# Two edits in a two-layer transformer kernel: the table of expert slots made on PE with gathered rows, and two gate groups of the LSTM's second block made at its entry

## The reference, cut to what matters

```python
gates = softmax(tokens @ wg)                        # 2048 x 8
expert_idx = argmax(gates)                          # one expert per token
pos = cumulative count of the token in its expert - 1
keep = pos < capacity                               # capacity 320 = 1.25 * 2048 / 8
y = gate * (relu(x @ w1[e] + b1[e]) @ w2[e] + b2[e])   # 0 for tokens that are not kept
out = residual + y
```

## Time and profile before

| | us |
|---|---|
| median of 3 runs (737.61 to 740.12) | 737.67 |
| profiled execution | 740.06 |
| its span, first to last instruction | 738.0 |
| PE busy | 683.7 (93%) |
| DVE busy | 437.1 (59%) |
| ACT busy | 343.8 (47%) |
| POOL busy | 132.9 (18%) |

### The profile page before, as it was taken

One profiled execution on the slowest core, in us unless ns is written; L12 is line 12 of the kernel. 1 busy time (PEld: TensorE's weight loads), 2 busy tenths in 40 slices (PEclk: granted clock), 3 DMA queues, 4 the chain that ended last, 5 costly groups with the idle time before them and its releaser, 6 DMA issues.

```text
span 738.0 us, 16775 instructions
## 1 busy us (share of the span) xinstructions
PE 683.7 (93%) x6616; PEld 573.8 (78%) x6625; DVE 437.1 (59%) x1152; ACT 343.8 (47%) x938; POOL 132.9 (18%) x220
## 2 busy tenths in 40 slices
PE   6699999999999999979999998999999999798992
PEld 2487778888889988867776776899999999434772
DVE  5499857748756657699999996333343444400321
ACT  1589852333222222378888885355554544101331
POOL 3225730140000000043000010000000000061576
PEclk8899999999999999999999998999999999789997
DMA  7600300000000000124222000000000000213222
GB/s 245 187 20 17 133 2 1 1 1 1 1 1 1 1 1 1 47 67 94 67 70 77 25 4 2 2 1 1 1 3 1 1 2 1 57 40 91 18 20 20
DMA packets 30007, 24.46 MB, mean 33 GB/s; under 512 B 3826, under 2 KB 27123, under 8 KB 29555
## 3 DMA queue, kind: packets, MB, share of 16 engines
q1 hardware_dynamic: 26482, 21.40, 10.2%
q0 software_dynamic: 3456, 2.12, 2.1%
HBM read 17.96 MB, written 5.80 MB: 32 GB/s over the span
## 4 chain that ended last, share of the span: by engine, by line
PE 81%; DVE 9%; issue 4%; SPq 3%; ACT 2%; DMA 1%; POOL 0%; POOLq 0%; DVEq 0%; ACTq 0%
PE SC L670 15%; PE PT L680 12%; PE MI L597 5%; PE SC L854 5%; PE PT L587 5%; PE SC L524 4%; PE SC L578 3%; PE SC L775 3%; PE SC L946 2%; PE SC L814 2%; PE SC L778 2%; PE SC L819 2%; PE PJ L560 2%; PE SC L781 2%; PE PT L825 2%
## 5 line engine op out<-in xcount | busy, mean ns | idle before, releaser
L1066 ACT ACTIVATE big<-SC 128x512 f32<-128x512 f32 x88 | 52.5, 598 | 144.3 <-PE SC L670 144.3
L680 PEld LDWEIGHTS PT<-wd,big 128*128 128x128 f32 (+1 forms) x768 | 90.2, 191 | 2.5 <-issue 0.4
L680 PE MATMUL PT<-wd,big 128*128 128x128 f32 (+1 forms) x768 | 90.6, 274 | 0.0
L1401 DVE TENSOR_TENSOR big<-SC,big 128x512 f32<-128x512 f32 (+1 forms) x88 | 60.5, 689 | 41.6 <-PE SC L670 32.3
L670 PE MATMUL SC<-xP,wgP 128*128 128x512 f32 x264 | 78.8, 406 | 0.7 <-DVE big L1401 0.3
L670 PE MATMUL SC<-xP,wuP 128*128 128x512 f32 x264 | 74.4, 390 | 0.0
L597 PEld LDWEIGHTS MI<-vblk,PTs 128*64 128x64 f32 x1536 | 49.8, 139 | 11.1 <-ACT oT L1013 2.8
L670 PEld LDWEIGHTS SC<-xP,wuP 128*128 128x128 f32 x264 | 49.5, 188 | 10.8
L597 PE MATMUL MI<-vblk,PTs 128*64 128x18 f32 x1536 | 54.2, 213 | 3.9 <-ACT big L1018 1.7
L524 PE MATMUL SC<-warm 128*128 128x512 bf16 x169 | 46.9, 432 | 9.5 <-DVE guess L1204 4.7
L1008 ACT ACTIVATE PTs<-PT 128x512 f32<-128x512 f32 x96 | 52.2, 595 | 7.6 <-PE PT L587 6.5
(11 more groups left out here) (227 smaller groups left out, 1323.1 us busy)
## 6 DMA issues: line engine op xcount, KB each, us to landing
kvs<-in_ctxT SPq DMA_DIRECT2D x32, 64.0 KB, 2.0
w1s<-in_e1w SPq DMA_DIRECT2D x8, 256.0 KB, 2.8
w2s<-in_e1w SPq DMA_DIRECT2D x8, 256.0 KB, 3.1
wg<-in_wg SPq DMA_DIRECT2D x1, 1408.0 KB, 9.2
wu<-in_wu SPq DMA_DIRECT2D x1, 1408.0 KB, 12.1
slots_in<-big SPq DMA_DIRECT2D x1, 1300.0 KB, 5.3
big<-slots_in SPq DMA_DIRECT2D x8, 130.0 KB, 2.4
wd<-in_wd SPq DMA_DIRECT2D x2, 512.0 KB, 14.2
```

The source lines that it names most:

```text
L680: last = pe.matmul(PT[:, e % 2, t * P:t * P + P], h[0:w, t * P:t * P + P], wd[0:w, e, c, :], start=(c == 0), stop=(c == 2))
L1066: act.activation(sg[a % 2], SC[:, a % 2, :], ACT.Silu).then_inc(s["silu_done"], 1)
L1401: last = dve.tensor_tensor(hT[e % 2][0:w, c, :], SC[0:w, 2 + a % 2, :], sg[a % 2][0:w, :], ALU.mult)
```

## The change: what it does

**Second block's gates.** At the entry PE also makes groups 0 and 1 of block 1, in the banks `PT[:, 0]` and `PT[:, 1]`, where six warming matmuls stood. ACT copies them in step 0. Step 1 makes group 2 and step 2 group 3, like all other blocks. In step 0 two warming matmuls go.

**Table of slots.** The slot number minus an offset is split in two: its block of 128 (`in_block`, a one-hot over `NQ` = 20 blocks) and its lane in the block (`at_lane`, a one-hot over 128 lanes, 16 tiles in four pieces of four). POOL multiplies `in_block` by the token's number (minus 4096) and by its gate. Then for each of 16 tiles PE multiplies the transposed lanes by those 20 columns and sums in one bank: the result at (lane, block) is the number of the token in that slot. An empty slot comes out as 4096, which is out of range. DVE turns it into the integer table `home` [128, 20]. The same product with the gates gives `gate` [128, 20].

**Gather.** SP stores X and XN side by side (2 x 128 wide) into `rows_in` in HBM, in token order, as each of the four groups is finished. POOL gathers 20 blocks of 128 slots by `home` with one indirect DMA each; every expert has two and a half blocks (`parts_of`: an even expert ends, an odd one begins with half a block). The gathered tiles lie in spent weights of the first mixture. `slots_in`, its zeros and all waits on them are gone.

**Experts.** Three parts per expert as before; for an odd expert the first part has 64 rows in the partitions 64 to 127, and the relu output is shifted by 64 columns, so that PE makes a full 128-row product for it. The residual row stands beside the gathered one. DVE adds gate x b2 to it ahead of time, and then gate x product, so ACT's `y_scale` is gone. The result overwrites the token's row in `out`: 20 indirect DMAs, one per block, that do not accumulate. The last expert's parts are made in three banks of `SC`, and each goes on by itself.

```diff
@@ SP
-            sp.wait_ge(s["zero_ready"], 1)
-            sp.dma_start(slots_in.rearrange("(p r) d -> p (r d)", p=P), zeros).then_inc(s["zero_stored"], 16)
...
-            sp.wait_ge(s["f_added"], NT)
+            rows_steps = rows_in.rearrange("(b i l) d -> l b i d", b=B, l=4)
+            for a, (lo, hi) in enumerate(GROUPS):
+                sp.wait_ge(s["f_added"], hi)
+                for l in range(4):
+                    sp.dma_start(rows_steps[l][:, lo:hi, D:2 * D], X[32 * l:32 * l + 32, lo:hi, :]
+                                 ).then_inc(s["rows_stored"], 16)
+                sp.wait_ge(s["ln_xn"], 3 * GRP + a + 1)
+                for l in range(4):
+                    sp.dma_start(rows_steps[l][:, lo:hi, 0:D], XN[32 * l:32 * l + 32, lo:hi, :]
+                                 ).then_inc(s["rows_stored"], 16)
...
@@ POOL
-            pool.memset(zeros, 0.0).then_inc(s["zero_ready"], 1)
...
-            for i in range(NT):
-                pool.indirect_dma_start(slots_in, bass.IndirectOffsetOnAxis(ap=slot[:, i:i + 1], axis=0),
-                                        XN[:, i, :], None, bounds_check=NSLOT - 1, oob_is_err=False
-                                        ).then_inc(s["scattered"], 16)
+            pool.memset(hE[1][:, 2:NF, 0:64], 0.0).then_inc(s["lead_ready"], 1)
+            pool.wait_ge(s["block_ready"], 1)
+            pool.tensor_tensor(token_at, in_block, token[:, :].unsqueeze(2).broadcast_to([P, NT, NQ]), ALU.mult
+                               ).then_inc(s["token_ready"], 1)
+            pool.tensor_tensor(gate_at, in_block, v1[:, :].unsqueeze(2).broadcast_to([P, NT, NQ]), ALU.mult
+                               ).then_inc(s["gate_ready"], 1)
+            pool.wait_ge(s["rows_stored"], 2 * 64 * len(GROUPS))
+            pool.wait_ge(s["home_ready"], 1)
+            for q in range(NQ):
+                pool.indirect_dma_start(xin[q], None, rows_in,
+                                        bass.IndirectOffsetOnAxis(ap=home[:, q:q + 1], axis=0),
+                                        bounds_check=T - 1, oob_is_err=False).then_inc(xin_loaded[q * P // CAP], 16)
             pool.wait_ge(s["out_stored"], 64)
             for e in range(E1):
-                p = e % 2
-                pool.wait_ge(s["y_ready"], e + 1)
-                for c, (_, w) in enumerate(SL):
-                    pool.indirect_dma_start(out, bass.IndirectOffsetOnAxis(ap=home[0:w, e, c:c + 1], axis=0),
-                                            yo[p][0:w, c, :], None, bounds_check=T - 1, oob_is_err=False,
-                                            compute_op=ALU.add).then_inc(y_added[p], 16)
+                for j, (q, _, _, w) in enumerate(parts_of(e)):
+                    if e % 2 == 1 or w == P:
+                        pool.wait_ge(s["y_ready"], 3 * e + j + 1)
+                        pool.indirect_dma_start(out, bass.IndirectOffsetOnAxis(ap=home[:, q:q + 1], axis=0),
+                                                xin[q][:, D:2 * D], None, bounds_check=T - 1, oob_is_err=False
+                                                ).then_inc(y_written, 16)
@@ PE
-            keep_warm(PT[:, 0, :], 6)
+            for g in range(2):
+                gate_x(PT[:, g, 0:P], 1, g)
+                gate_src(PT[:, g, 0:P], 1, g)
+                gate_tgt(PT[:, g, 0:P], 1, g)
...
-                if t in (1, 2):
-                    gate_in(1, 2 * t - 2)
-                    gate_in(1, 2 * t - 1)
-                elif t == 0:
-                    keep_warm(PT[:, 0, :], 2)
+                if t == 0:
+                    pass
...
-            pe.wait_ge(s["slots_ready"], 1)
-            with pe.Fori(0, 4) as _:
-                keep_warm(SC[:, 3, :], BURST)          # BURST = 28
+            pe.wait_ge(s["token_ready"], 1)
+            for i in range(NT):
+                if i % 4 == 0:
+                    pe.wait_ge(s["lane_ready"], i // 4 + 1)
+                last = pe.matmul(MI[:, 0:NQ], at_lane[:, i, :], token_at[:, i, :], start=(i == 0), stop=(i == NT - 1))
+            last.then_inc(s["home_summed"], 1)
+            pe.wait_ge(s["gate_ready"], 1)
+            for i in range(NT):
+                last = pe.matmul(PJ[:, 0:NQ], at_lane[:, i, :], gate_at[:, i, :], start=(i == 0), stop=(i == NT - 1))
+            last.then_inc(s["gate_summed"], 1)
+            keep_warm(SC[:, 3, :], BURST)              # BURST = 10
+            pe.wait_ge(s["lead_ready"], 1)
@@ DVE, after v4
-            dve.tensor_scalar(slot[:, :], v4[:, :], NOWHERE, None, ALU.add).then_inc(s["slots_ready"], 1)
+            link(dve.tensor_scalar(v2[:, :], v4[:, :], 1.0 / P, TO_BLOCKS, ALU.mult, ALU.add))
+            link(dve.tensor_scalar(v3[:, :], v2[:, :], TO_BLOCKS, None, ALU.subtract))
+            dve.tensor_tensor(in_block, ..., ALU.is_equal).then_inc(s["block_ready"], 1)
+            link(dve.scalar_tensor_tensor(v3[:, :], v3[:, :], -float(P), v4[:, :], ALU.mult, ALU.add))
+            for i in range(0, NT, 4):
+                dve.tensor_tensor(at_lane[:, i:i + 4, :], ..., ALU.is_equal).then_inc(s["lane_ready"], 1)
+            dve.wait_ge(s["home_summed"], 1)
+            dve.tensor_scalar(home[:, :], MI[:, 0:NQ], NO_TOKEN, None, ALU.add).then_inc(s["home_ready"], 1)
+            dve.wait_ge(s["gate_summed"], 1)
+            dve.tensor_copy(gate[:, :], PJ[:, 0:NQ]).then_inc(s["gate_kept"], 1)
@@ DVE, expert, after its two relus
+                for q, r, _, w in parts_of(e):
+                    y = xin[q][r:r + w, D:2 * D]
+                    dve.scalar_tensor_tensor(y, b2r[r:r + w, e, :], gate[r:r + w, q:q + 1], y, ALU.mult, ALU.add
+                                             ).then_inc(s["y_biased"], 1)
+                dve.wait_ge(s["y_biased"], 3 * e + 3)
+                for j, (q, r, _, w) in enumerate(parts_of(e)):
+                    y = xin[q][r:r + w, D:2 * D]
+                    dve.wait_ge(s["e2_done"], 3 * e + (j + 1 if e == E1 - 1 else 3))
+                    dve.scalar_tensor_tensor(y, y_bank(e, j)[r:r + w, :], gate[r:r + w, q:q + 1], y,
+                                             ALU.mult, ALU.add).then_inc(s["y_ready"], 1)
```

More of the change, by code:

```diff
@@ L127, in build @@
             "p (i e j) -> p i e j", i=NT, e=NR) for i in range(2))
-        xin = [big[:, i * 3 * DR:(i + 1) * 3 * DR].rearrange("p (c d) -> p c d", c=3) for i in range(E1)]
-        zeros = big[:, 0:NSLOT * DR // P]
         warm = sb("warm", [P, 512], mybir.dt.bfloat16)
@@ L181, in build @@
         v1, v2, v3, v4 = (sb(f"v{i}", [P, NT]) for i in range(1, 5))
-        slot = sb("slot", [P, NT], U32)
         token = sb("token", [P, NT])
-        home = sb("home", [P, E1, 3], U32)
+        home = sb("home", [P, NQ], U32)
+        gate = sb("gate", [P, NQ])
         th = [sb(f"th{i}", [P, 4, B]) for i in range(2)]
@@ L208, in build @@
         base = spent[0:1, 5 * P:7 * P]
+        lanes, blocks = spent[:, 9 * P:10 * P], spent[:, 10 * P:10 * P + NQ]
+        in_block, token_at, gate_at = (spent[:, a * P:a * P + NT * NQ].rearrange("p (i q) -> p i q", i=NT)
+                                       for a in (11, 14, 17))
+        dead_u = wu[:, :, :].rearrange("p e k -> p (e k)")
+        xin = ([dead_u[:, 256 * q:256 * q + 256] for q in range(11)]
+               + [wd[:, e, 0:2, :].rearrange("p c d -> p (c d)") for e in range(E0)] + [spent[:, 7 * P:9 * P]])
         xsT = [sb(f"xsT{i}", [P, CAP]) for i in range(2)]
@@ L211, in build @@
         w2s = sb("w2s", [P, E1, NF, D])
-        hE = [sb(f"hE{i}", [P, NF, CAP]) for i in range(2)]
+        hE = [sb("hE0", [P, NF, CAP]), sb("hE1", [P, NF, 64 + CAP])]
         xn_last = hE[1][:, :, :].rearrange("p c t -> p (c t)")[:, 0:512].rearrange("p (t d) -> p t d", t=4)
-        yo = [sb(f"yo{i}", [P, 3, D]) for i in range(2)]
         SC = psum("SC", [P, RG, 512])
@@ L240, in build @@
         xin_loaded = [sem(f"xin_loaded{i}") for i in range(E1)]
-        y_added = [sem(f"y_added{i}") for i in range(2)]
+        y_written = sem("y_written")
         N_CONST, N_ATTN, N_MOE, N_LATE, N_LSTM = 10, 1, 5, 6, 2
@@ L834, in rows_t @@
                     bank = PT[:, 1, (i - lo) * P:(i - lo) * P + P] if i - lo < 4 else PJ[:, 0:P]
-                    last = pe.transpose(bank, XN[:, i, 0:D], ident[:, :])
+                    last = pe.transpose(bank, XN[:, i, :], ident[:, :])
                 last.then_inc(s["rows_transposed"], 1)
@@ L930, in expert_in @@
             def expert_in(e, p):
[L932 removed]
+                pe.wait_ge(xin_loaded[e], 32 if e % 2 else 48)
                 wait(pe, s["xin_copied"], e - 1)
[L934 to L935 removed]
+                for q, r, o, w in parts_of(e):
+                    last = pe.transpose(PT[:, p, o:o + w], xin[q][r:r + w, 0:D], ident[r:r + w, r:r + w])
                 last.then_inc(s["xin_transposed"], 1)
@@ L975, in _ @@
         def _(act):
-            act.wait_ge(s["zero_ready"], 1)
-            act.activation(rs[0][:, 0:1], zeros[:, 0:1], ACT.Exp)
+            act.wait_ge(s["warm_ready"], 1)
```

(6 more changed lines are left out.)

123 lines of the change are left out of this document (57 added, 66 removed).

## The result

The changed kernel took 734.21 us (median of 7 runs, 732.37 to 735.95) against 739.51 (7 runs, 737.61 to 741.72) for the kernel before: a ratio of 0.9927, with a 95% interval of 0.9907 to 0.9947. It is faster by 5.3 us. The forecast was 720.1, 17.6 us faster, with a range of 713 to 725; it was too low by 14 us.

What follows compares the result with a forecast made beforehand. The prediction took PE's chain of waits (81% of the span) as the bound. Its terms -3.2 - 8.8 + 0.5 - 6.1 gave -17.6 from the median 737.67, so 720.1 us, range 713 to 725.

Steps and rivals of the forecast that it cites:

- LSTM entry, -3.2: LSTM's first steps: steps 1 and 2 hold one gate group each, and two warming matmuls go; 3.2 us saved.
- Start and stores: Kernel start and SP's row stores: dropping zeros gains nothing, and the 32 row stores were counted as costing nothing.
- Table at the lower clock, 6.7 us a product: Table of slots: PE makes all of it at 1.2 GHz, 6.7 us each for `home` and the gates.
- Rival A: Table of slots: the clock rises inside it and gathers then bind; -23.7 us, 714.0 us, chance 0.2.
- PE's own order, not the gather, starts the experts: Before expert 0: PE's gates and warming end at 667.2, after the third gather's landing at 663.1.
- Gather step 1.28: POOL's gathers: each 1 KB-row gather takes 1.28 us, like a plain scatter, with 1.89 as upper bound.
- B: POOL's queue: every indirect DMA costs 1.85 us; -6.4 us, 731.3 us, chance 0.08.
- D: POOL's single queue becomes the bound, 20 gathers ahead of every scatter; +1.8 us, 739.5 us, chance 0.05.
- C: Table: POOL's product is held until DVE finishes `at_lane`, 2.6 us later; -15.0 us, 722.7 us, chance 0.05.
- Tail -6.1: After PE's last product: its thirds finish separately, ending at T+6.2 against T+12.3 (T = PE's end); 6.1 us saved.
- Hand-over, -8.8 + 0.5: From slots to ACT's copy for expert 0: 8.8 us earlier, less 0.5 for a late clock rise (bounds 0 and 2).
- The experts... 49.3, kept: Experts, from ACT's first copy to PE's last product: same PE work per expert, so 49.3 us unchanged.

Runs made afterwards that it cites:

- e11: Changed kernel with 24 more wide warming matmuls in PE's two waits ahead of the table (14 and 10): 718.99 us, ratio 0.9745.
- e5: Changed kernel, unaltered, measured again in the second session: 723.98 us, ratio 0.9806 to the kernel before.
- e6: Changed kernel with gathers 0 to 8 writing the old down and gate weights, 9 to 19 the old up weights: 723.97 us, ratio 0.9804.
- e8: Changed kernel with the old LSTM entry, leaving the table, gathers and new output scatters: 727.10 us, ratio 0.986.
- e9: Changed kernel, unaltered, measured again in the third session: 721.97 us, ratio 0.9787 to the kernel before.
- e17: Changed kernel gathering rows of 512 bytes instead of 1024, residual half left out, sixth session: 722.86 us, ratio 0.979.
- e18: Changed kernel, unaltered, one run in the sixth session: 723.0 us.
- e3: Changed kernel with gathers 0 to 8 writing the old down and gate weights, 9 to 19 the old up weights; first session, one run: 726.66 us.
- e4: Changed kernel gathering rows of 512 bytes instead of 1024, residual half left out; first session, one run: 723.98 us.
- e16: Changed kernel, unaltered, one run in the fifth session: 737.53 us.
- e1: Changed kernel with only eight gathers issued in a row, those of expert e + 3 waiting until PE finished expert e: 724.57 us, ratio 0.9813.

## Why the prediction was wrong

- **LSTM entry, -3.2**: right. -2.6 in times, -2.9 and -3.1 in traces (-4.3 in the first trace of the changed kernel, where the clock fell to 1.2 GHz 2.4 us before the one-hot and not 5.6 to 7).
- **Start and stores**: nothing of them shows, as far as the scatter of 4 us ahead of the LSTM lets one see.
- **Table at the lower clock, 6.7 us a product**: right. Rival A came about only when e11 put wide matmuls ahead of it, and for one product of the two.
- **"PE's own order, not the gather, starts the experts"**: right; the warming is followed by the transposes with no DMA wait.
- **Gather step 1.28**: 1.31. Rivals B and D fell with it. C did not come as written: `token_at` took 0.73 us and was not held. But what it named did happen the other way round, DVE's first lane piece took 1.24 us instead of the 0.69 forecast, and the table starts 0.55 us later by it.
- **Tail -6.1**: -5.7.
- **Hand-over, -8.8 + 0.5**: too large by 2 us where there is no hold. The new length is nearly as forecast (21.5 us; 29.4 - 8.3 = 21.1), and the lane piece makes up the difference. The old one had been read from a trace whose hand-over was 1.5 us longer than in the next, with the pause in it. I had booked the distance of that trace from the median (2.4 us) as lying in other stretches. The 0.5 for the clock was 0 in the six traces of the changed kernel and its nearest variants without a hold (e5, e6, e8, e9, e17, e18), and 1.7 in e3 and e4, where the clock rose 3.9 us after the first copy: within the bounds of 0 and 2.
- **"The experts... 49.3, kept"** is the step that failed. It was 61.6 (47.9 without a hold; the kernel before has 49.0 by the same measure). The forecast put the wait for PE's counts at nothing; it was 11.7 us for PE, and the lower clock behind it cost 2 more. I asked whether PE would wait for gathers and whether DVE would be late; I did not ask whether the counts that engines send each other would still arrive at once with twenty indirect transfers beside the experts. The trace had no such pair: its scatters ran beside matmuls for which nobody waits, and the later ones in groups of three.

Where there is no hold the three sessions gave 722.0, 723.0 (a single run) and 724.0, inside the range of 713 to 725, and the sum of the traces is -16.1 for -17.6. Where there is, the change keeps a quarter to a third of that (5.3 and 3.7 us; a single run, e16, kept 1.7). The forecast could not know the place, but the path on which it lost the time is one that it had declared free.

Not settled: what makes a place hold. Each result names its chip by a number, and number 4 was a place without a hold in the first session (its variants, by the mark) and with one in the fifth, so it is more than that number. Nor is it shown what is held. That PE's increments are recorded late, while PE itself goes on to 671.5 and ACT and DVE stand still, fits a delay on their way. The pause in the old burst, where nobody is waited for, would rather say that PE itself can be stopped; whether the two are one thing is open. So is how much of this is the recording: every run lists a granted clock and so was recorded, and landings are missing from the record at just these places. A rival that no run here excludes is that the hold exists only in executions that are recorded.

## What to carry to other kernels

When a change lets a long row of indirect transfers run beside work in which engines wait for each other every microsecond, don't price it by the engines' orders alone: issue only what the next stages need, and keep the rest behind them. That halved the loss here (12.1 to 6.3 us) and cost nothing that shows where there was none (e1 at 724.6, the unaltered kernel at 724.0 in the next session). Run the unaltered kernel again in each session before a variant is credited with a cure; four different edits "cured" this hold because the session had none. When the profiled run lies 2 us from the median, look first at where these 2 us are: in one trace of the kernel before 1.5 us lay in the stretch that the change removes, in the other, 2.6 us above its median, they lay ahead of the LSTM. And two-operand work on DVE and POOL side by side is not free: keep the piece that PE waits for out of it.

## What the hardware showed

- The clock beside the table: in the first trace PE ran the table from 644 to 658 at 0.50 and it rose in the warming behind, at 660 to 662; in e11 it fell from 1.00 at 650 to 652, in the middle of the table. The Trainium skill ("TensorE: Matmul & The Clock Gate", Part 1) says that sustained activity releases the gate. Neither row agrees, taken alone: PE was busy for 13.67 of 14.00 us in the first and without a gap in the second.
- A plain indirect scatter or gather with 128 rows holds POOL 1.0 us, an accumulating scatter 1.4 to 1.6. The size of the row does not show: gathers with rows of 1 KB (e9) and of 512 bytes (e17) both took 1.00 us.
- DVE's and POOL's two-operand work side by side slow each other: 1.24 and 1.21 us instead of 0.68 for DVE's 512 elements, 1.17 against 0.73 for POOL's 320. The Trainium skill ("GPSIMD Engine Reference", Key points) says that POOL shares its SBUF interfaces with DVE and contends with DVE instructions that have two SBUF inputs; the trace agrees, and 0.55 us of it were on the path. With a gather it was less: one of 1.09 us among those of 1.00, issued at 665.83 in the first trace, beside DVE's fused operations.
